# Router products moved to the next step, an expert register kept, and a second result bank for small tiles

## What is computed

```python
# attention: x = layernorm(x)
Wh = x @ W
e = leaky_relu((Wh @ a[:256])[:, None] + (Wh @ a[256:])[None, :], 0.2)
alpha = softmax(where((adj > 0) | eye(N), e, -9e15), axis=1)
x = x + alpha @ Wh
# experts, on xt = layernorm(x): 8 experts, 2 for each row
logits = xt @ Wr + br
top_p, top_idx = top_k(softmax(logits), 2)
weights = top_p / top_p.sum(-1)
xn = layernorm(xt) * ln_g[e] + ln_b[e]
y = gelu(xn @ W1[e] + b1[e]) @ W2[e] + b2[e]      # W1: 256x1024, W2: 1024x256
x = x + (weights * y of the two experts).sum()
```

## Time and profile before

| | us |
|---|---|
| median of 3 runs (993.95 to 996.27) | 993.97 |
| the profiled execution | 993.66 |
| its span, first to last instruction | 991.9 |
| PE busy in the span | 948.2 |
| DVE busy in the span | 790.4 |

### The profile page before, as it was taken

One profiled execution on the slowest core, in us unless ns is written; L12 is line 12 of the kernel. 1 busy time (PEld: TensorE's weight loads), 2 busy tenths in 40 slices (PEclk: granted clock), 3 DMA queues, 4 the chain that ended last, 5 costly groups with the idle time before them and its releaser, 6 DMA issues. The chain is left out here.

```text
span 991.9 us, 22957 instructions
## 1 busy us (share of the span) xinstructions
PE 948.2 (96%) x7550; PEld 797.4 (80%) x7551; DVE 790.4 (80%) x1210; ACT 613.7 (62%) x900; POOL 635.0 (64%) x632
## 2 busy tenths in 40 slices
PE   4999999999999999999999999999999999999994
PEld 3888999889988898889888977777777777777762
DVE  7689998999999999999999446787666676577653
ACT  3789898878888887878786544334333433333441
POOL 5312251295875865847729458888888888888652
PEclk9999999999999999999999999999999999999998
DMA  8548879787888697886877986443332332232321
GB/s 276 98 160 233 294 230 273 220 234 251 249 247 294 184 296 227 251 248 196 262 252 202 360 340 205 92 111 60 60 55 44 49 58 43 43 54 42 45 34 22
DMA packets 92236, 170.97 MB, mean 172 GB/s; under 512 B 19952, under 2 KB 69360, under 8 KB 83824
## 3 DMA queue, kind: packets, MB, share of 16 engines
q1 hardware_dynamic: 58384, 134.07, 40.4%
q0 software_dynamic: 24048, 26.23, 16.9%
q10 hardware_dynamic: 9712, 9.45, 3.4%
HBM read 136.91 MB, written 41.19 MB: 180 GB/s over the span
## 5 line engine op out<-in xcount | busy, mean ns | idle before, releaser
L1130 ACT ACTIVATE hf<-tp,b_cols 128x256 f32<-128x256 f32 (+1 forms) x312 | 116.2, 459 | 177.0 <-PE tp L882 174.3
L774 PE MATMUL acc<-wh,pt_hi 128*128 128x256 f16 x768 | 209.4, 273 | 0.0
L775 PE MATMUL acc<-wh,pt_hi 128*128 128x256 f16 x768 | 209.4, 273 | 0.0
L776 PE MATMUL acc<-wh,pt_lo 128*128 128x256 f16 x768 | 209.4, 273 | 0.0
L552 POOL TENSOR_TENSOR x_late<-x_late,wsp 128x1024 f32<-128x1024 f32 x32 | 78.8, 2463 | 170.0 <-DMA x_late<-in_L_ffn_W 164.9
L898 PE MATMUL acc<-w_sb,h_hi 128*128 x568 | 171.1, 379 | 5.3 <-issue 3.9
L1279 DVE SCALAR_TENSOR_TENSOR sc<-t_row,s_col 128x2048 f32<-128x2048 f32 x64 | 162.6, 2541 | 8.6 <-PE tp L755 6.7
L658 POOL DMA_INDIRECT out<-y_sb,yidx x71 | 121.7, 1714 | 66.7 <-DVE y_sb L1602 39.6
L880 PE MATMUL tp<-x_hi,w_sb 128*128 128x256 f16 (+1 forms) x624 | 161.3, 264 | 1.9 <-ACT hf L1130 1.8
L882 PE MATMUL tp<-x_down,w_sb 128*128 128x256 f16 (+1 forms) x624 | 161.4, 264 | 0.0
L881 PE MATMUL tp<-x_lo,w_sb 128*128 128x256 f16 (+1 forms) x624 | 161.0, 263 | 0.0
(11 more groups left out here) (240 smaller groups left out, 1787.8 us busy)
## 6 DMA issues: line engine op xcount, KB each, us to landing
adj_sb<-in_adj SPq DMA_DIRECT2D x64, 1024.0 KB, 7.4
x_late<-in_L_ffn_W SPq DMA_DIRECT2D x32, 512.0 KB, 9.8
wsplit_dram<-wsp SPq DMA_DIRECT2D x32, 512.0 KB, 8.9
w_sb<-wsplit_dram SPq DMA_DIRECT2D x32, 512.0 KB, 8.9
xs<-rows_dram ACTq DMA_DIRECT2D x32, 260.0 KB, 3.4
wsp<-in_L_ffn_W POOLq DMA_DIRECT2D x32, 256.0 KB, 4.8
x<-in_x SPq DMA_DIRECT2D x32, 128.0 KB, 9.6
out<-x SPq DMA_DIRECT2D x32, 128.0 KB
```

Of the source, the lines that this page charges most:

```text
L774: pe.matmul(o, pt_hi[g][:, cols], wh[:, j, 0, :], start=(j == 0), stop=False)
L775: pe.matmul(o, pt_hi[g][:, cols], wh[:, j, 1, :], start=False, stop=False)
L776: m = pe.matmul(o, pt_lo[g][:, cols], wh[:, j, 0, :], start=False, stop=False)
```

## The change

Three edits. In the router, `normalise` is split over q = 1 and q = 2, two tiles each; `router_t(b, 1)` goes from the middle to the end of PE's step q = 2; ACT's `router(b, 1)` goes to step q = 3 between the first two `p_hi`; `router_mm(b, 1)` goes from the end of q = 2 into q = 3, behind product 3 of the tile before; `router_pos` goes to the end of q = 3. In the experts' tiles that are written out, `down` uses the register that `up` has loaded. Small tiles take the banks `acc[0]` and `acc[1]` in turn, and `down` waits only for the result before the last one.

```diff
+        def bank_of(t):
+            return (t - NB) % 2 if isinstance(t, int) and t >= NB else 0
...
                 if i > 0:
                     av(i - 1, 1 - u, 2)
                     av(i - 1, 1 - u, 3)
+                if in_batch(b) and q == 3:
+                    router_mm(b, 1)
                 if in_batch(b) and q == 2:
                     router_t(b, 0)
...
                 if in_batch(b) and q == 2:
                     router_mm(b, 0)
-                    router_t(b, 1)
-                if in_batch(b) and q == 3:
-                    router_pos(b)
                 if now:
                     p_transpose(i, u, 3)
                     av(i, u, 1)
                 if in_batch(b) and q == 2:
-                    router_mm(b, 1)
+                    router_t(b, 1)
+                if in_batch(b) and q == 3:
+                    router_pos(b)
...
+            experts = {}
             def up(t, first=0, last=HC):
-                e = expert_of(t)
+                e = experts[t] if first > 0 else expert_of(t)
+                if isinstance(t, int):
+                    experts[t] = e
...
             def down(t, u):
-                e = expert_of(t)
+                e = experts.pop(t) if isinstance(t, int) and t in experts else expert_of(t)
+                a = bank_of(t)
                 pe.wait_ge(s_hh, t + 1)
-                if within(t, 1, FT):
+                if within(t, NB + 1, FT) and isinstance(t, int):
+                    pe.wait_ge(s_yc, total(t - 1, 2))
+                elif within(t, 1, FT):
                     pe.wait_ge(s_yc, total(t, 2))
...
-                        pe.matmul(acc[s][:, :], h_hi[u][:, (c * ns + s) * P:(c * ns + s + 1) * P], w_both,
+                        pe.matmul(acc[s + a][:, :], h_hi[u][:, (c * ns + s) * P:(c * ns + s + 1) * P], w_both,
...
                     p_hi(i, 0)
                     if i == 0:
                         wh_hi(NP - 1)
+                    if in_batch(b) and q == 3:
+                        router(b, 1)
                     p_hi(i, 1)
...
-                if in_batch(b) and q == 1:
-                    for k in range(RB):
+                if in_batch(b) and (q == 1 or q == 2):
+                    for k in range(2 * (q - 1), 2 * q):
                         normalise(b, k)
                 if in_batch(b) and q == 2:
                     router(b, 0)
...
-                if in_batch(b) and q == 2:
-                    router(b, 1)
```

More of the change, by code:

```diff
@@ L897, in down @@
                     for s in range(ns):
-                        pe.matmul(acc[s][:, :], h_hi[u][:, (c * ns + s) * P:(c * ns + s + 1) * P], w_both,
+                        pe.matmul(acc[s + a][:, :], h_hi[u][:, (c * ns + s) * P:(c * ns + s + 1) * P], w_both,
                                   start=(c == 0), stop=False, skip_group_check=True)
                     for s in range(ns):
-                        m = pe.matmul(acc[s][:, 0:D], h_lo[u][:, (c * ns + s) * P:(c * ns + s + 1) * P], w_hi,
+                        m = pe.matmul(acc[s + a][:, 0:D], h_lo[u][:, (c * ns + s) * P:(c * ns + s + 1) * P], w_hi,
                                       start=False, stop=(c == HC - 1), skip_group_check=True)
@@ L1593, in result @@
                 for s in range(ns):
-                    dve.scalar_tensor_tensor(out=y[:, s, :], in0=acc[s][:, D:2 * D], scalar=1.0 / LOSCALE,
+                    dve.scalar_tensor_tensor(out=y[:, s, :], in0=acc[s + a][:, D:2 * D], scalar=1.0 / LOSCALE,
                                              in1=b2_rep[:, bass.ds(e * D, D)], op0=ALU.mult, op1=ALU.add).then_inc(s_yc, 1)
@@ L1597, in result @@
                 for s in range(ns):
-                    dve.tensor_tensor(y[:, s, :], acc[s][:, 0:D], y[:, s, :], ALU.add).then_inc(s_yc, 1)
+                    dve.tensor_tensor(y[:, s, :], acc[s + a][:, 0:D], y[:, s, :], ALU.add).then_inc(s_yc, 1)
                 dve.wait_ge(s_yc, total(t + 1, 2))
```

## The result

The changed kernel took 1004.19 us (median; 1002.7 to 1004.61), the kernel before in the same session 994.38. The ratio is 1.009, 95% interval 1.0059 to 1.012: slower by 0.9%. The profiled execution took 1004.1 us, its span is 1002.3 us. The forecast was 1004.0.

The account below looks back on a forecast made before the run. PE (62.78 of 64.22 us a batch) and DVE (61.70) were both taken as nearly full, DVE setting the pace afterwards. 993.66 + 14.4 (six rounds) - 4.4 (register) + 0 (bank) = 1003.7, median 1004.0; range 995.5 to 1010 us.

Parts of the forecast that it names:

- The new wait: DVE at q = 3 waits for the logits from `router_mm(b, 1)`: 3.5 us of forced idle, against 2.5 to give.
- DVE's round: DVE's pieces over a batch's four steps: 64.2 us now, 65.4 plus the q = 3 collision afterwards.
- the 67.1 of the working: Forecast length of one batch on DVE: 65.4 plus 1.7 us for the q = 3 collision.
- the worked 2.9: Growth of a batch to 67.1 us; lowered to a mean of 2.4 for slack in the two early batches.
- The collision at q = 1: DVE against POOL's weight split, 1.97 us today: kept, with the split waiting for `scores` and the masks for the split.
- The collision at q = 3: DVE's `scores` or gap against POOL's weight split after the logits: taken at 1.7 us, bounds 0 and 2.1.
- The rival that it hides there wholly: POOL's split falls in DVE's wait for the logits and costs nothing: +2.6 us, 996.6 in all; chance 0.12.
- The waits that go: PE's router waits, 10.8 us over seven batches, go (one-hots' wholly), but PE waits for `p_lo` instead; counted inside the round.
- The register: Register load before `down` in small tiles: seven gaps go, -4.4 us taken, between 3.2 and 4.8; nothing in big tiles.
- The second bank: The 1.3 us wait before the last `down` goes, but POOL's last result gains nothing: 0, bounds 0 and -1.3.
- The sum: 993.66 + 14.4 - 4.4 = 1003.7 us for the profiled execution; the median 0.3 higher, so 1004.0.

Follow-up runs that it names:

- the held split: POOL's weight split held until DVE has finished the next step's masks: 981.68 us in the kernel before, 985.7 us in the changed kernel.
- The experiment with the transposes first: Changed kernel with the router product before product 3 and, in small tiles, tile t+2's transposes ahead of up(t+1): 987.83 us, ratio 0.9923.
- the move alone: Kernel before with only the second half of the router's products moved behind product 3 in the next step: 1012.95 us, ratio 1.0163.

## Why the prediction was right

The range held and the time came out within 0.2 us. The mechanism, DVE's wait for the logits in a round that DVE fills, is shown. That the number fits so well is partly luck, as the steps show:

- *The new wait.* Priced at 3.5 us a round (1.12 to 4.67 from `p_lo` 0 to the logits). The piece measured 3.83 to 4.59 over the seven batches, 4.21 in the one walked, so it grew by 2.7 to 3.5. Moving the product away alone gave back 14 us. Shown.
- *DVE's round.* The pieces of the changed kernel in batch 4, by the starts of its `p_lo` 0 (392.35, 407.00, 423.43, 438.54, 458.90): q = 0 14.65 (forecast 15.45), q = 1 16.43 (16.19), q = 2 15.11 (14.7), to the logits 4.21 (4.67), from there 16.15 (16.07 with the collision). The sum is 66.55 against the 67.1 of the working; q = 0 lost a collision on `choose_rows` that I had taken for fixed work, 0.8 us. The mean of the six rounds is 66.8, 2.4 us more than before, and 2.4 were forecast. But the 2.4 was the worked 2.9 less an allowance for slack in the two early batches, and that slack did not show: from `p_lo` 0 to `p_lo` 0 the first two rounds grew by 2.9 and 3.7 us. The mean came from the third and the sixth, which grew by 0.9 and 0.8. This is luck.
- *The collision at q = 1.* I had it moved from `scores` to what follows. That is what happened: POOL's split started at 415.20, while `scores` ran, and the diagonal behind `scores`, 0.2 us of work, took 2.16.

```profile
414.40 2.35 DVE L1291 SCALAR_TENSOR_TENSOR sc<-t_row,s_col 128x2048 f32<-128x2048 f32 x1
416.67 2.16 DVE L1307 TENSOR_TENSOR bias_sb<-bias_sb,off_diag 128x128 bf16<-128x128 bf16 x1
```

- *The collision at q = 3.* Taken at 1.7, bounds 0 and 2.1. It fell on `scores` in steps 7 and 23 (4.27 and 4.10 us), on the gap in step 15, on the logits' bias in the other three; in none of the six rounds was it 0; it cost 1.0 to 1.9 us. In step 19 the split started 0.01 us after the logits arrived:

```profile
376.20 0.19 DVE L1352 TENSOR_TENSOR lg<-rt_ps,g 128x32 f32<-128x32 f32 x1 [2.82 <-PE rt_ps L802]
376.43 1.96 DVE L1355 TENSOR_TENSOR lg<-lg,b_r_rep 128x32 f32<-128x32 f32 x1
```

Only in step 27 did the split begin inside the wait, at 510.77, 0.76 us before the logits could be read, and the bias still had to wait for its end. The rival that it hides there wholly did not come about; that without a collision the change would be nearly free is borne out only in part: with the held split it still costs 1.1 us a round.
- *The waits that go.* I wrote that the wait for the one-hots would go wholly. It fell from 4.8 to 2.2 us, as the one-hots come late too. PE also gained a wait of 2.5 us for ACT's copy that I had not priced.
- *The register*, -4.4 us: the step that was mis-sized. The seven gaps before `down` went, but the small tiles gained 2.9 us, less than the 3.2 of my lower bound, and a tile between two small ones became 0.3 us shorter, not 0.65. With `down` 0.7 us earlier, `up` waits 0.4 us for its x split in five tiles; so it had 0.3 us to spare before. I had not asked what is late next. The experiment with the transposes first showed it.
- *The second bank*, 0: measured 0.
- *The sum.* The register gave 1.5 us less than forecast. The attention outside the six rounds gave back 0.7 us and the big tiles 0.3, neither of them forecast. So +10.4 stands beside +10.0 in the profiled executions.

What I had wrong without its touching the number is the reading of the kernel before. I took both PE and DVE as nearly full and the collisions as fixed parts of DVE's round. Part of DVE's 61.70 us in the earlier trace rows was DVE standing still for POOL: with the split held, DVE is busy for 58.0 us of a batch of 62.35 and PE for all of it, with none of the waits for one-hots and `p_lo` left.

## What to carry to other kernels

Before a product is moved later, ask which instruction on another in-order engine reads it, and what is queued behind that reader; eight matmuls of 0.8 us, put 3.5 us too late in each of seven batches, cost 14 us. When PE waits longer, look at the granted clock too: in the move alone it fell to half after the waits, and the transposes behind them took nearly twice as long. Where an engine is over 95% busy, look for instructions that take twice their usual time beside another engine's, and time the other engine's work under those that read PSUM: one wait added on an engine with slack was worth more than the whole router order. A saved instruction in a short tile is worth only as much as the next wait in the loop leaves.

## What the runs showed of the hardware

A subtraction of four numbers a row on DVE can cost 1.9 us instead of 0.15, if POOL's 128 x 1024 subtraction began first; by the Trainium skill, page "SBUF — State Buffer", section "Who interferes with whom", two SBUF inputs against a GpSimd read suffice for that, and the trace agrees. `p_lo`, with one input in PSUM, ran at 1.20 us beside the same split, and placing the split there took 13 us off the kernel before (994.45 to 981.68). An indirect DMA's issue on POOL took 4.47 us in the changed kernel, from 419.82 on, across DVE's mask pass of 419.00 to 423.42; one at 449.78, with no such pass under way, took 0.98:

```profile
419.82 4.47 POOL L596 DMA_INDIRECT rows_dram<-rows,slot  x1 [0.30 <-issue]
```

So a pass with two SBUF inputs holds up this instruction too: it ends 0.87 us after the pass, and so does the one at 447.28 after the `scores` of step 23 above (449.47 against 448.60). The Trainium skill, in the same section, infers that making descriptors needs only the write side of the shared pair, which a `tensor_tensor` leaves free; for this instruction the measurement says otherwise. Whether it is held in making descriptors or in reading its slots, which lie in SBUF, no run here separates.
